# A LayerNorm row sum computed by a ScalarE Copy with an accumulator instead of a VectorE reduction, in a fused attention and feed-forward layer

## What is computed

```python
qkv = (x @ W_qkv + b_qkv)                      # 16 heads of 64
q = _layernorm(q, q_gamma, q_beta)             # per head
k = _layernorm(k, k_gamma, k_beta)
scores = einsum(q, k) / 8                      # causal, window of 512
out = softmax(scores) @ v
attn = out @ W_out + b_out
x = _layernorm(x + attn)                       # mean, variance over 1024
xn = x * rsqrt(mean(x * x) + 1e-6)             # RMS norm
xq = round(xn * 127 / absmax) / (127 / absmax) # 8-bit rounding
y = xq @ (w_int8 * weight_scale).T + bias
x = _layernorm(x + y)                          # mean, variance over 1024
```

## Time and profile before

| what | us |
|---|---|
| median of 2 runs | 1786.62 (1786.3 to 1786.94) |
| the profiled execution | 1787.37 |
| its span on the slowest core | 1785.6 |
| spans of the 8 cores | 1780.9 to 1785.6 |
| TensorE busy (matmul) | 847.4 |
| VectorE busy | 970.3 |
| ScalarE busy | 420.3 |
| GpSimd busy | 343.7 |

### The profile page before, as it was taken

The page is one execution under the profiler, slowest core; times in us unless marked ns, Lnnn a source line. Parts: engine busy times, 40 slices in busy tenths (PEclk is TensorE's granted clock), DMA queues, the critical chain, the costliest instruction groups (busy, mean ns, idle before and its releaser), DMA issues.

```text
span 1785.6 us, 20934 instructions; the slowest of 8 cores (1780.9 to 1785.6 us)
## 1 busy us (share of the span) xinstructions
PE 847.4 (47%) x5096; PEld 427.1 (24%) x5096; DVE 970.3 (54%) x1953; ACT 420.3 (24%) x945; POOL 343.7 (19%) x281
## 2 busy tenths in 40 slices
PE   0126555454454636445463555546455554545521
PEld 0012222122222213222232323223122222332310
DVE  2125655555737374563837556473754647474544
ACT  0001122222223132232313223131222312332221
POOL 0000011121213122231212213021221302242200
PEclk9997666667575765657576575756657575656565
DMA  9420000000100001010000101001010000000000
GB/s 153 93 81 6 1 7 7 12 7 1 30 1 24 7 1 31 1 30 1 19 12 1 30 1 31 1 3 28 1 30 1 25 0 1 25 24 1 25 12 24
DMA packets 11807, 35.10 MB, mean 20 GB/s; under 512 B 1322, under 2 KB 1450, under 8 KB 11690
## 3 DMA queue, kind: packets, MB, share of 16 engines
q0 software_dynamic: 4480, 12.59, 4.5%
q1 hardware_dynamic: 7210, 21.17, 3.5%
HBM read 37.97 MB, written 8.39 MB: 26 GB/s over the span
## 4 chain that ended last, share of the span: by engine, by line
DVE 46%; PE 27%; issue 11%; ACT 7%; DMA 3%; DVEq 2%; another core or an unknown queue 2%; POOL 1%; ACTq 0%; SPq 0%; POOLq 0%
PE big L331 8%; PE big L819 5%; PE ptp L186 4%; DVE probsT L196 4%; PE big L849 3%; DMA rci<-w 3%; PE avp L476 2%; ACT probs L444 2%; DVE zzb L349 2%; DVE arena L359 2%; DVE fence L172 2%; DVE arena L351 2%; DVEq L48 2%; DVE negC L437 2%; DVE hb L645 2%
## 5 line engine op out<-in xcount | busy, mean ns | idle before, releaser
L450 POOL TENSOR_TENSOR probs<-probs,mask4s 128x640 bf16<-128x640 bf16 (+4 forms) x256 | 330.7, 1292 | 1185.7 <-ACT probs L444 1174.7
L186 PE MATMUL ptp<-idents,probs 128*128 128x128 bf16 x1120 | 160.7, 302 | 402.1 <-DVE probsT L196 188.4
L331 PE MATMUL big<-wqkvb,xfm 128*128 128x512 bf16 x768 | 224.8, 459 | 55.8 <-DVE vtm L713 33.0
L186 PEld LDWEIGHTS ptp<-idents,probs 128*128 128x128 bf16 x1120 | 100.4, 129 | 488.7 <-issue 488.4
L196 DVE COPY probsT<-ptp 128x640 bf16<-128x640 bf16 (+4 forms) x256 | 115.2, 450 | 78.2 <-PE ptp L186 54.4
L819 PE MATMUL big<-woutb,afm 128*128 128x512 bf16 x256 | 89.7, 513 | 116.7 <-DVE afm L196 116.7
L476 PE MATMUL avp<-vtm,probsT 128*128 128x65 bf16 x1120 | 106.7, 241 | 58.0 <-ACT araw L489 28.4
L444 ACT ACTIVATE probs<-scp,negC 128x640 bf16<-128x640 f32 (+4 forms) x128 | 93.3, 729 | 158.9 <-DVE fence L172 130.6
L331 PEld LDWEIGHTS big<-wqkvb,xfm 128*128 128x128 bf16 x768 | 85.1, 115 | 183.9 <-issue 134.1
L444 ACT ACTIVATE probs<-big,negC 128x640 bf16<-128x640 f32 (+4 forms) x128 | 93.3, 729 | 108.3 <-DVE fence L172 91.4
L356 ACT ACTIVATE sqqk<-zzb 128x1024 bf16<-128x1024 bf16 x32 | 33.8, 1057 | 347.4 <-DVE zzb L349 347.4
(11 more groups left out here) (119 smaller groups left out, 1237.6 us busy)
## 6 DMA issues: line engine op xcount, KB each, us to landing
xres<-x SPq DMA_DIRECT2D x16, 512.0 KB, 4.5
out<-x1b SPq DMA_DIRECT2D x16, 512.0 KB, 2.9
wqkvb<-wqkv POOLq DMA_DIRECT2D x1, 6144.0 KB, 43.5
rci<-w SPq DMA_DIRECT2D x16, 256.0 KB, 2.8
xbf<-x POOLq DMA_DIRECT2D x16, 256.0 KB, 4.2
woutb<-wout POOLq DMA_DIRECT2D x1, 2048.0 KB, 55.5
mask4s<-mask SPq DMA_DIRECT2D x1, 160.0 KB
idents<-ident SPq DMA_DIRECT2D x1, 32.0 KB
```

The source lines that it names most:

```text
L186: fn = lambda e, src=src, c=c: e.transpose(ptb[:, c * 128:(c + 1) * 128], src, ident.ap())
L331: OP("tensor", lambda e, l=lhs, r=rhs, ps=ps, kk=kk: e.matmul(ps, l, r, start=(kk == 0), stop=False))
L450: e.tensor_mul(pb[:, 0:w], pb[:, 0:w], mask4.ap()[:, moff:moff + w]))
```

## The change

In t1 the VectorE reduction over the row is removed. In its place ScalarE runs a second pass over the same row tile, a Copy with an accumulator, between the Square and the fence. It writes the copied row into the scratch tile `ry`, over the squares that nothing reads, and its accumulator puts the row sum into column 0 of `lar`. The fence on which t2 waits now stands behind both passes. The two waits of VectorE for pc stay, and now stand ahead of whatever VectorE runs next. `ln_stats_thunks` is called for both chains of all 16 tiles, so the edit acts 32 times.

```diff
--- before.py
+++ after.py
@@ -538,11 +538,12 @@
                 INC("scalar", "sAC", lambda e: e.activation(
                     out=ry.ap(), in_=src_sb.ap(), func=AF.Square,
                     accum_out=L[:, 1:2]))
+                INC("scalar", "sAC", lambda e: e.activation(
+                    out=ry.ap(), in_=src_sb.ap(), func=AF.Copy,
+                    accum_out=L[:, 0:1]))
                 G["rysq"] = FAC()
                 for fn in x1b_gates:
                     fn()
-                INC("vector", "sDV", lambda e: e.tensor_reduce(
-                    out=L[:, 0:1], in_=src_sb.ap(), axis=AX.X, op=ALU.add))
 
             def t2():
                 W("vector", "sAC", G["rysq"])
```

## The result

The changed kernel took 1813.06 us (median of 7 runs, 1812.26 to 1814.24), the kernel before 1786.91 us (6 runs, 1786.3 to 1787.85). The ratio is 1.0146 with a 95% interval of 1.0134 to 1.0159. So the change made the kernel 26.1 us, or 1.5%, slower. That lies under the 2% from which a difference was to be called one, and clear of the noise. The prediction was 1807 us with a range of 1799 to 1818. The profiled execution took 1811.81 us.

What follows compares the result with a forecast made beforehand. An order of waits, not a full engine, was taken to bound the kernel (VectorE 54% busy). 17.5 - 3.7 + 6.25 = 20.0 us on 1787.37 gave 1807.4, or 1806.6 against the median; forecast 1807 us, range 1799 to 1818.

Steps and rivals of the forecast that it cites:

- TensorE's clock: Shifted rounds change where the granted clock rises in projection waves: 0 in the sum, 4 us either way.
- The price of a pass: Added price c of one ScalarE Copy with accumulator ahead of the fence: 1.25 us, bounds 0.20 and 1.31.
- First kind: pc with attention around it, 14 places: reduction hidden behind ScalarE's Square, so the whole pass is paid, 17.5 us.
- the stalls stay: Rival: at fc with attention the mask starts before L555, one stall of about 1.2 us each: 1821.6 us; 8 in 100.
- Second kind: fc with attention around it, 13 places: 16.25 us paid, less 5.8 of margins and 14.1 of stalls: -3.7 us.
- Third kind: Five places in the last rounds without attention: the whole pass is paid, 6.25 us.
- The rival that it turns against the change in every round: TensorE's clock costs 1.1 us more in each of 14 rounds, adding 15 us: 1822 us; 7 in 100.
- The formula, 32 c - 20.0: Whole change: each of 32 places pays the added price c; margins and stalls give back 20.0 us.
- A cheap second pass: Rival: the ScalarE pass costs below 0.63 us, kernel no slower; 1773.8 us at the 0.20 bound; 4 in 100.
- VectorE's relief reaching the end: Rival: VectorE gains 1.22 us and a 0.1 gap at 32 places, ScalarE's pass free: 1745 us; 1 in 100.
- The signs: Profile after: Copy 1.06 us, idle ahead of L549 about 90, VectorE busy down 53, ScalarE up 40, attention rounds 105.8.

Runs made afterwards that it cites:

- the runs with added instructions: Four or five one-column VectorE fences a round added to the kernel before, behind the q normalization: 1801.13 us with four, 1809.23 us with five.
- the one-input runs: L553 and L555 written with one SBUF tensor input and a per-partition scalar: 1773.15 us from the kernel before, 1808.24 us from the changed kernel.

## Why the prediction was right, and what it missed

The mechanism held at all 32 places: steps of 20.6 us there, for a forecast of 20.0. The measured time lies 6 us over the predicted one. In the profiled execution 4.5 us of it are there (24.5 for 20.0), and most of them are a term that the sum had at nothing, TensorE's clock; the rest is spread between executions. That the time lies inside the range all the same is due to the room that the range left for that clock.

**The price of a pass.** Put at c = 1.25 us from the Square beside it. It measured 2.48 - 1.25 = 1.23 us in the two places shown, and twice the Copy gave 1.26 us of further idle time a place. The bounds of 0.20 and 1.31 weren't needed.

**First kind, 17.5 us.** Right in mechanism: the lag grew by 1.23 us at each place, 17.3 in all, and nearly none came back. The run with the Copy in pc alone cost 18.5 us beside the clock for 14 + 2 places, 20.0 by the formula. The run with both reduction and Copy shows the other half, that the removed reduction was worth nothing there. One thing was missed. The 0.13 us by which L555 keeps ahead of the mask is as thin as I said, and in one of the 14 places of the changed kernel L554 came 0.35 us late, and L556 then started behind the mask and waited it out, 1.4 us in the lag with what followed.

```profile
1379.10 0.16 DVE L554 TENSOR_TENSOR lar<-lar 128x1 f32<-128x1 f32 x1 [0.46 <-DVE lar L552]
1379.15 1.39 POOL L450 TENSOR_TENSOR probs<-probs,mask4s 128x640 bf16<-128x640 bf16 x1 [2.26 <-ACT probs L444]
1379.37 1.19 DVE L556 TENSOR_TENSOR lar<-lar 128x1 f32<-128x1 f32 x1
```

This is what the rival "the stalls stay" feared, in one place of 32 and not in the second kind. With it the stalls gave back 12.6 us over all.

**Second kind, -3.7 us.** Right in mechanism and nearly in size: 10.0 us of waits for 10.5 and 14.2 us of stalls given back for 14.1, so -4.3 us. For fc alone the sum said 0.1 us and the run 5.2 (3.7 from the first Square on). The stalls left in L560, 2.7 us where I had counted on 0.7, explain 2.0 of it; the rest is not settled.

**Third kind, 6.25 us.** Right. From the Square of the last fc with attention around it to the last Square of all the lag grew by 4.8 us (four pairs of 1.25, less the fc's small gain), and by 1.3 behind that.

**TensorE's clock, 0 in the sum and 4 us either way.** This is the term that was off. It came to +3.3 us in 11 rounds, +3.4 in the lined-up traces, and with the stall of 1.4 us it is nearly all that lies between the predicted 20.0 and the measured 24.5 us of the profiled execution. The spread of 4 us was too narrow: beside the 354.8 of the kernel before, the slowest cores of four of the other eleven kernels have 5 to 9 us more. As a price of longer rounds it isn't to be had: the runs with added instructions refute that. What decides which waves run at the lower level stays open; cores with the same program differ in it, and these traces don't let me forecast it. The rival that it turns against the change in every round at 1.1 us (1822) did not happen.

**The formula, 32 c - 20.0.** Tested at three values of c: 0 gave -20.1 us (formula -20.0), 1.24 gave +26.1 (+19.7), and 2.5 gave +63.0 (+60). At the 32 places themselves the lined-up traces give -19.1, +20.6 and +60.8 us, so slope and offset hold there. Over the whole kernel the agreement at 0 is partly luck. From the first Square on, less the stretch and in the median of the cores, the three are -15.5, +21.6 and +61.6 us: without reduction and Copy some 3.6 us were lost again elsewhere in the rounds, and why is not settled.

**The rivals on the other side.** A cheap second pass falls with the 1.056 us of the Copy. VectorE's relief reaching the end falls with the run without a sum: with all 32 reductions gone and nothing in their place, 20 us came at most, not 42. The Trainium skill, page "Perfetto Trace Analysis", section "Optimizing Scalar/DVE Operations", allows the offload where VectorE is saturated; at 54% of the span, and with 23.2 us of waiting at the very place, this trace did not meet that condition. The page "SBUF — State Buffer" of the Trainium skill, section "Who interferes with whom", was confirmed by the one-input runs: without the second tensor input no instruction of the two groups stalled behind the mask.

**The signs.** VectorE busy fell by 52.7 us (53 forecast), the idle time ahead of t2 rose to 95.7 (about 90, though the prediction's own terms give 95 or more), the Copy took 1.06. The attention rounds grew from 104.8 to 106.1 us, 1.3 each where 1.0 was forecast; 0.3 of it is the clock's stretch. ScalarE busy rose by 35.0 and not 40, mostly because the accumulator read starts 0.1 us before its Copy has ended.

## What to carry to other kernels

Before work is moved from a busy engine to an idle one, look at what the next reader waits for. If the idle engine's result comes last there, the move lengthens the path by the whole new pass and the old engine's saved time turns into waiting; here 39 us of VectorE work were worth nothing once the Copy stood on ScalarE. A sum over a row was cheapest here in the accumulator of the instruction that writes the row (0.08 us). And a one-column instruction with two tensor inputs cost as much as the 128x640 multiply of another engine that it started behind (1.39 us), so where it starts, or how many tensor inputs it has, is worth more than its width.

## What the runs showed of the hardware that was not expected

The form with a per-partition scalar took 0.214 us on one column, the form with two tensor inputs 0.160, and the form with a constant 0.154. The accumulator on VectorE's 128x1024 add cost 0.08 us and did not slow the add (1.224 us). The stretch of TensorE waves between the attention's normalization and the q cast, nearly the same work in all kernels here, ranged from 31.0 to 35.5 us a round on the slowest cores, a wider spread than the 2.2 us that two whole rounds of the kernel before had shown. So a change of a few us in this kernel can't be told from the way the clock falls without the timeline of the waves.
